# SiLU as one ScalarE function over several strips in the convolutions, the MLP and a gate of a two-layer vision state-space network

## The chip, the cores and the metric

The kernel runs on one core of one Trainium2 chip. The metric is the device time of one execution in microseconds (us), as the median of several executions. Engines are named as in the profile: PE is TensorE's matmul unit and PEld its weight load, DVE is VectorE, ACT is ScalarE, POOL is GpSimd, and SP is the engine that issues the DMAs.

## What is computed

The input is a batch of 8 images of 64x64 positions with 192 channels, all in f32. Two layers follow each other.

- **Layer 0**: a linear projection to 384 + 384 channels; on the first half a 3x3 depthwise convolution and SiLU; a state-space scan in two directions in chunk form, done by matmuls; a gate SiLU(z) of the second half; an output projection with residual; then an MLP 192 -> 768 -> 192 with SiLU between, and a residual.
- **Layer 1**: the first 96 channels go through two 3x3 convolutions and a 1x1 convolution with ReLU. The other 96 are layer-normed and projected to `xi` and `z`, 192 channels each; `xi` has a 3x3 depthwise convolution and SiLU; a selective scan in four directions with 16 states a channel; a layer norm, a gate SiLU(z), and a projection back.

```python
def _silu(v):
    return v * jax.nn.sigmoid(v)
...
xi = jax.nn.silu(_conv(xi, conv2d_w, conv2d_b, groups=D_INNER))
...
def step(h, t):
    u_t, d_t, b_t, c_t = t
    h = jnp.exp(d_t[..., None] * A) * h + (d_t * u_t)[..., None] * b_t[:, :, None, :]
    return (h, jnp.einsum('bkdn,bkn->bkd', h, c_t))
...
yv = _ln(yv, out_norm_g, out_norm_b) * jax.nn.silu(z)
```

SiLU stands in five places: after each of the two depthwise convolutions, in the gate of layer 0, in the MLP and in the gate of layer 1.

## The kernel before

**Rounds.** The work is a pipeline over the 8 images. A round holds up to three parts: `pre` of one image (layer 0 and the preparation of layer 1's scan: stages a to f), `scan` of the image before it (layer 1's selective scan: stage s), and `fin` of the image before that (stages g and h: sum of directions, norm, gate, output projection). There are ten rounds: one with `pre` alone, one with `pre` and `scan`, six in the middle with all three, one with `scan` and `fin`, one with `fin` alone. Between rounds all engines meet at a barrier (`clear`) and semaphores are set to zero.

**The scan** is 384 units of 128x1024 a round. For a unit ACT takes the exponential of the step (`dA<-dA,A`), PE spreads the input over the states into one of two PSUM buffers (`PU<-PT,SELB`), DVE multiplies it by B (`PU<-PU,BR`) and runs the recurrence as a scan instruction (`H<-dA,CR,PU`, line 1738), ACT copies the last state for the chunk that follows (`CR<-H`), POOL multiplies by C (`HC<-H,BR`) and PE sums over the states (`PY<-HC,CB`). The spreading of unit u+1 waits for the scan of unit u-1, since it takes the same half of `PU` (`s_expand`).

**Stages of `pre`.** They work on 8 strips of 512 positions. a: transposes, input projection, and the depthwise convolution, of which PE does six taps (`a.conv`), ACT two (`side_taps`) and DVE one and the merge (`merge_taps`); then SiLU, and from it the tokens (transposes and a projection, `a.tokens`). b: layer 0's chunked scan. c: gate, output projection, and the MLP (`c.mlp`, six blocks of 128 hidden channels a strip, then `c.mlp2`). d: the three convolutions of layer 1. e: norm, `in_proj` (`e.inproj`) and the depthwise convolution (`e.conv`). f: step sizes by softplus and their products.

**The order.** Every engine executes its own fixed list. Generators (`pipeline`, `woven`) write the list of steps of `pre` and `fin`; the table `TAKEN` then says for each kind of round and engine how many of these steps stand behind each third of a scan slot (`merged`). So where a step stands among the scan units is a number in that table, and a late operand holds up all that is behind it on its engine. In a middle round `pre` and `fin` have two PSUM banks for one another's matmuls and evictions at a time (`Round`).

**SiLU before.** v times sigmoid(v) is written as h·(1 + tanh h) with h = v/2. Weights and biases are halved once (`WH`, `DV0`). In the depthwise convolutions ACT computes tanh of `T1` into `T0` (`conv_tanh`), and DVE combines both (`a_silu`, `e_silu`). In the MLP and in layer 1's gate ACT reads the PSUM bank twice, for tanh and for h (`c_mlp`, `e_inproj`), and DVE combines:

```python
act(K.MA[m % 2], pb[:, :], ACT.Tanh, bias=K.DV0[:, 18 + j:19 + j], scale=0.5)
act(K.MB[m % 2], pb[:, :], ACT.Identity, bias=K.DV0[:, 18 + j:19 + j], scale=0.5).then_inc(S["c_hact"], 1)
...
stt(K.HB[i % 2][j], K.MA[m % 2], 1.0, K.MB[m % 2], ADD, MUL).then_inc(S["c_hs"], 1)
```

Layer 0's gate (`c_gate`) has the same form; there DVE multiplies with PSUM directly.

## Time and profile before

| | |
|---|---|
| median of 3 runs | 19261.31 us (19232.4 to 19284.86) |
| profiled execution, its own time | 19287.62 us |
| its span | 19285.8 us |
| PE busy | 14729.8 us, 76% |
| DVE busy | 15816.2 us, 82% |
| ACT busy | 8249.6 us, 43% |
| POOL busy | 10174.2 us, 53% |
| granted TensorE clock, mean | 0.826 of full speed |

Busy times are sums over the whole span, and the rounds have different limits; so a stage is read from its own stretch. A matmul's end is modelled, and a busy PE isn't PE at its peak. The idle time in front of an instruction is put down to what was seen to end it.

### The profile page before, as it was taken

Reading aid. Unit: us, or ns where it says so; the run is one execution under the profiler, and the core shown is the slowest. Engines: PE = TensorE matmul, PEld = TensorE weight load, DVE = VectorE, ACT = ScalarE, POOL = GpSimd, SP = SyncE. Lnnn points to the kernel's source line nnn. Section 1 sums busy time; section 2 is a strip of 40 time slices with the busy share of each in tenths; the row PEclk is TensorE's granted clock in tenths of the full one; section 3 lists DMA queues with packets and bytes.
Section 4 is the critical chain, followed back from the end, with each engine's and each line's share of the span. In section 5 each row is a group of like instructions: output and inputs, shape, how many; then the busy total and the mean of one; then the engine's idle time right before and its main releaser. Section 6 shows DMA issues by size and latency. Waiting matters only on the chain. (4 is left out here: it accounts for less than half of the span.)

```text
span 19285.8 us, 212341 instructions
## 1 busy us (share of the span) xinstructions
PE 14729.8 (76%) x65784; PEld 6341.4 (33%) x65784; DVE 15816.2 (82%) x12143; ACT 8249.6 (43%) x14280; POOL 10174.2 (53%) x5172
## 2 busy tenths in 40 slices
PE   7886789677886788767886878867788678874554
PEld 4433433233332333234332343324333233321102
DVE  3327989689887988979888798988988798898994
ACT  3244334543355334643346433454335533463332
POOL 2115755466455654547455574456645565454662
PEclk9988888788988889888977888878898888975555
DMA  2226666566765667666675666666766566757774
GB/s 80 85 75 174 179 180 168 162 174 186 176 167 166 180 180 187 169 163 182 170 194 163 170 183 177 176 172 174 189 175 167 169 179 180 188 166 175 185 183 113
DMA packets 1556889, 3220.31 MB, mean 167 GB/s; under 512 B 289936, under 2 KB 721872, under 8 KB 1554256
## 3 DMA queue, kind: packets, MB, share of 16 engines
q1 hardware_dynamic: 1555792, 3206.72, 62.4%
q8 instruction: 561, 9.19, 0.2%
q14 instruction: 536, 4.39, 0.1%
HBM read 2474.94 MB, written 731.12 MB: 166 GB/s over the span
## 5 line engine op out<-in xcount | busy, mean ns | idle before, releaser
L1887 POOL TENSOR_TENSOR HC<-H,BR 128x1024 f32<-128x1024 f32 x3072 | 7380.3, 2404 | 5919.5 <-DVE H L1738 3717.3
L1738 DVE TENSOR_TENSOR_SCAN H<-dA,CR,PU 128x1024 f32<-128x1024 f32 x2304 | 5400.1, 2344 | 375.9 <-ACT CR L1119 166.8
L789 PE MATMUL PU<-PT,SELB 96*128 96x512 bf16 x6144 | 2280.3, 460 | 3097.3 <-DVE H L1738 2536.4
L1119 ACT ACTIVATE dA<-dA,A 128x1024 f32<-128x1024 f32 x3072 | 3508.6, 1143 | 2306.2 <-DMA dA<-dld 2280.4
L1482 DVE TENSOR_TENSOR PU<-PU,BR 128x1024 f32<-128x1024 f32 x3072 | 3731.2, 1215 | 411.5 <-PE PU L789 390.3
L789 PE MATMUL PB<-RA,RB 128*128 128x64 f32 (+3 forms) x9120 | 2804.8, 456 | 76.2 <-DVE RA L1485 65.1
L789 PE MATMUL PY<-HC,CB 128*32 128x256 f32 x24576 | 2397.2, 469 | 72.0 <-POOL HC L1887 51.2
L789 PEld LDWEIGHTS PU<-PT,SELB 96*128 96x128 bf16 x6144 | 505.2, 104 | 4675.4 <-issue 4065.7
L1738 DVE TENSOR_TENSOR_SCAN H<-dA,PU 128x1024 f32<-128x1024 f32 x768 | 1755.0, 2285 | 141.1 <-ACT dA L1119 49.3
L789 PEld LDWEIGHTS PB<-RA,RB 128*128 128x128 f32 (+2 forms) x9120 | 1394.6, 188 | 1307.7 <-issue 1173.8
L789 PE MATMUL PB<-RA 128*128 128x384 f32 (+2 forms) x4272 | 1758.1, 551 | 9.0 <-ACT RA L1119 9.0
L1119 ACT ACTIVATE YS<-PY 128x256 f32<-128x256 f32 x768 | 293.2, 382 | 2344.4 <-PE PY L789 2282.7
L789 PEld LDWEIGHTS PB<-RA 128*128 128x128 f32 (+1 forms) x4272 | 870.0, 213 | 944.9 <-issue 762.5
L789 PE MATMUL PB<-RB 96*128 96x128 bf16 (+2 forms) x6624 | 853.3, 260 | 391.5 <-ACT RA L1119 333.2
L789 PE MATMUL PB<-RA,PX 96*128 96x512 f32 x2304 | 1125.3, 629 | 19.4 <-issue 16.0
L1119 ACT ACTIVATE CR<-H 128x1 f32<-128x1 f32 x3072 | 598.0, 195 | 1218.4 <-DVE H L1738 1211.6
L789 PEld LDWEIGHTS PY<-HC,CB 128*32 128x32 f32 x24576 | 530.9, 118 | 1732.5 <-issue 1546.8
L1119 ACT ACTIVATE RA<-PB 128x384 f32<-128x384 f32 (+2 forms) x1736 | 752.9, 457 | 712.9 <-PE PB L789 470.9
L1809 POOL TENSOR_TENSOR T<-T,PX 128x512 f32<-128x512 f32 (+1 forms) x320 | 407.0, 1272 | 929.5 <-ACT PX L1119 929.2
L789 PE MATMUL PB<-XT,RB 96*128 96x512 f32 x1536 | 794.4, 656 | 87.8 <-issue 36.7
L789 PEld LDWEIGHTS PB<-RB 128*128 128x128 f32 (+1 forms) x6624 | 686.2, 153 | 501.4 <-ACT RA L1119 367.9
L1828 POOL TENSOR_TENSOR RA<-RA 128x768 f32<-128x768 f32 x344 | 505.8, 1470 | 594.5 <-PE PB L789 377.4
(174 smaller groups left out, 18145.8 us busy)
## 6 DMA issues: line engine op xcount, KB each, us to landing
dA<-dld SPq DMA_DIRECT2D x3072, 512.0 KB, 6.4
PT<-ptd SPq DMA_DIRECT2D x2304, 64.0 KB, 4.4
BR<-bcd SPq DMA_DIRECT2D x256, 512.0 KB, 7.4
ptd<-RA SPq DMA_DIRECT2D x176, 576.0 KB, 3.9
y0d<-RA SPq DMA_DIRECT2D x512, 192.0 KB, 7.8
RA<-y0d SPq DMA_DIRECT2D x128, 768.0 KB, 6.5
yd<-YS SPq DMA_DIRECT2D x768, 128.0 KB, 4.9
tkd<-RB SPq DMA_DIRECT2D x256, 262.0 KB, 4.8
```

Of the source, the lines that this page charges most:

```text
L789: return nc.tensor.matmul(out, w, x, start=start, stop=stop, skip_group_check=True)
L1119: return ac.activation(out, in_, f, **kw)
L1482: return v.tensor_tensor(out, a, b, op)
L1738: v.tensor_tensor_scan(h, a, x, 0.0 if first else K.CR[:, gi:gi + 1], MUL, ADD).then_inc(S["s_scan"], 1)
L1809: po.tensor_tensor(o, o, K.PX[0:P, strip(m % 3)], ADD).then_inc(S["side"], 1)
L1828: po.tensor_tensor(K.DX[u % 3].rearrange("p (w h q) -> p w h q", w=2, h=6), tk[:, xo:xo + 384].rearrange("p (h q) -> p h q", h=6).unsqueez ...
L1887: po.tensor_tensor(K.HC[:, w % NHC, :], K.H[:, w % NH, :], K.BR[:, (w // 24) % NBR, 1, :], MUL).then_inc(S["s_mulC"], 1)
```

## The change

In the two depthwise convolutions, the MLP and layer 1's gate, the halving is dropped, the pre-activation is written to SBUF whole, and one ACT instruction with the function Silu works in place or into its target over several strips: 1536 columns in stage a (the three channel blocks of a strip), 3072 in the MLP (its six blocks), 1024 in the gate (two blocks), 2048 in stage e (four strips). DVE's combining instructions are gone there. The consumers wait for one such instruction where they waited for three to six. Layer 0's gate stays as it was. Three DMAs of a strip's convolution output go out together behind its one Silu, and the gate's two DMAs become one. The tables of the order are others. The cut diff:

```diff
...
     ("first", "PE"): counts(
-        "0000000000000300300000000600000000600000600000600000600000600000G00900400100100h009006000001001f09005003101009"
...
+        "0000000000000300300000000600000000600000600000600000600000600000G00900400000200h00900600000200000o005003001001"
...
-    "tap": {"a": 24, "e": 16}, "half": {"a": 24, "e": 16}, "tanh": {"a": 24, "e": 16},
-    "silu": {"a": 24, "e": 16},
+    "tap": {"a": 24, "e": 16}, "half": {"a": 24, "e": 16}, "silu": {"a": 8, "e": 4},
...
-        "zo0": {"e": 128}, "zo1": {"e": 128},
+        "zo0": {"e": 64}, "zo1": {"e": 64},
...
-        self.XJ = [rb(512) for _ in range(3)]
+        self.XJS = rb(1536)
+        self.XJ = [self.XJS[:, j * 512:(j + 1) * 512] for j in range(3)]
+        self.TA = [t[:, :, :].rearrange("p j n -> p (j n)") for t in (T0, T1)]
...
-        self.HB = [[ra(512) for _ in range(6)], [PX[:, j * 512:(j + 1) * 512] for j in range(6)]]
+        self.HB = [ra(3072), PX[:, :]]
...
-        self.MA = [XI[:, i, :, :].rearrange("p a c -> p (a c)")[:, 0:512] for i in range(2)]
-        self.MB = [rb(512), ra(512)]
...
-        self.ZT = [ra(512, 96) for _ in range(2)]
-        self.ZO = [XI[0:96, i, :, :].rearrange("p a c -> p (a c)")[:, 0:512] for i in range(2)]
+        self.ZO = [XI[0:96, :, :, :].rearrange("p i a c -> p i (a c)")[:, :, 0:512],
+                   ra(1024, 96).rearrange("p (j n) -> p j n", j=2)]
...
-        pe.wait_ge(*R.at("silu", m + 1, "a"))
+        pe.wait_ge(*R.at("silu", m // 3 + 1, "a"))
...
-            pe.wait_ge(S["c_hs"], 6 * i + 6)
+            pe.wait_ge(S["c_hs"], i + 1)
...
-    def side_taps(ph, m, P, img, w, bias, i):
-        o = K.T1[0:P, m % 3, :]
+    def side_taps(ph, m, P, o, img, w, bias, i):
         o8 = K.PX[0:P, strip(m % 3)]
         if m >= 3:
-            ac.wait_ge(*R.at("silu", m - 2, ph))
-        act(rows8(o), tap_rows(img, i, 7), ACT.Identity, bias=bias, scale=K.WH[0:P, w + 7:w + 8])
-        act(rows8(o8), tap_rows(img, i, 8), ACT.Copy, scale=K.WH[0:P, w + 8:w + 9]).then_inc(S["taps"], 1)
-
-    def conv_tanh(ph, m, P):
-        ac.wait_ge(*R.at("half", m + 1, ph))
-        if m >= 3:
-            ac.wait_ge(*R.at("silu", m - 2, ph))
-        act(K.T0[0:P, m % 3, :], K.T1[0:P, m % 3, :], ACT.Tanh).then_inc(S["tanh"], 1)
+            ac.wait_ge(*R.at("side", m - 2, ph))
+        act(rows8(o), tap_rows(img, i, 7), ACT.Identity, bias=bias, scale=K.V[0:P, w + 7:w + 8])
+        act(rows8(o8), tap_rows(img, i, 8), ACT.Copy, scale=K.V[0:P, w + 8:w + 9]).then_inc(S["taps"], 1)
 
     def a_side(m, p):
         i, j = divmod(m, 3)
         if m == 0:
             ac.wait_ge(*R.at("rim", 1, "a"))
         ac.wait_ge(S["a_rows"], 3 * min(i + 1, 7) + 3)
-        side_taps("a", m, 128, K.XP[:, j], 9 * j, K.DV0[:, 15 + j:16 + j], i)
-
-    def a_conv(m, tap):
-        if tap == NTAP:
-            conv_tanh("a", m, 128)
+        if i >= 2:
+            ac.wait_ge(*R.at("silu", i - 1, "a"))
+        side_taps("a", m, 128, K.TA[i % 2][:, strip(j)], K.XP[:, j], W0 + 9 * j, K.vec("cb", j, P=128), i)
+
+    def a_silu(m, p):
+        i, j = divmod(m, 3)
+        if p or j < 2:
+            return
+        ac.wait_ge(*R.at("half", m + 1, "a"))
+        if i:
+            ac.wait_ge(S["a_tproj"], 4 * i)
+            for j in range(3):
+                ac.wait_ge(S[f"xj{j}"], 16 * i)
+        act(K.XJS, K.TA[i % 2], ACT.Silu).then_inc(S["silu"], 1)
...
     def c_mlp(i, j):
         m = 6 * i + j
-        pb = R.bank(("c.mlp", i, j))
+        if i >= 2:
+            ac.wait_ge(S["c_mlp"], 2 * (i - 2) + 2)
         ac.wait_ge(S["c_h"], m + 1)
-        if m >= 2:
-            ac.wait_ge(S["c_hs"], m - 1)
-        act(K.MA[m % 2], pb[:, :], ACT.Tanh, bias=K.DV0[:, 18 + j:19 + j], scale=0.5)
-        act(K.MB[m % 2], pb[:, :], ACT.Identity, bias=K.DV0[:, 18 + j:19 + j], scale=0.5).then_inc(S["c_hact"], 1)
+        act(K.HB[i % 2][:, strip(j)], R.bank(("c.mlp", i, j))[:, :], ACT.Identity,
+            bias=K.vec("b1", j, P=128)).then_inc(S["c_hact"], 1)
+        if j == 5:
+            ac.wait_ge(S["c_hact"], m + 1)
+            act(K.HB[i % 2], K.HB[i % 2], ACT.Silu).then_inc(S["c_hs"], 1)
...
-            m = 2 * i + e - 2
-            if m >= 2:
-                ac.wait_ge(S["e_z"], m - 1)
-                ac.wait_ge(S[f"zo{m % 2}"], 16 * (m // 2))
-            act(K.ZT[m % 2], pb[0:96, :], ACT.Tanh, bias=K.IPW[:, 4 + e:5 + e], scale=0.5)
-            act(K.ZO[m % 2], pb[0:96, :], ACT.Identity, bias=K.IPW[:, 4 + e:5 + e], scale=0.5).then_inc(S["e_zact"], 1)
+            zo = K.ZO[i % 2]
+            if i >= 2:
+                ac.wait_ge(S[f"zo{i % 2}"], 16 * (i // 2))
+            act(zo[:, e - 2, :], pb[0:96, :], ACT.Identity, bias=K.IPW[:, e:e + 1]).then_inc(S["e_zact"], 1)
+            if e == 3:
+                ac.wait_ge(S["e_zact"], 2 * i + 2)
+                act(zo, zo, ACT.Silu).then_inc(S["e_z"], 1)
 
     def e_side(m, p):
         j, i = divmod(m, 8)
         ac.wait_ge(S["e_rows"], 2 * min(i + 1, 7) + 2)
-        side_taps("e", m, 96, K.YP[:, j], 27 + 9 * j, K.DV0[0:96, 24 + j:25 + j], i)
-
-    def e_conv(m, tap):
-        if tap == NTAP:
-            if m == 0:
-                ac.wait_ge(S["e_p"], 32)
-            conv_tanh("e", m, 96)
+        if m == 0:
+            ac.wait_ge(S["e_xn"], 8)
+        side_taps("e", m, 96, K.C1[:, j, strip(i)], K.YP[:, j], W1 + 9 * j, K.vec("cdb", j), i)
+
+    def e_silu(m, p):
+        j, i = divmod(m, 8)
+        if i % 4 == 3:
+            x = K.C1[:, j, (i - 3) * 512:(i + 1) * 512]
+            ac.wait_ge(*R.at("half", m + 1, "e"))
+            act(x, x, ACT.Silu).then_inc(S["silu"], 1)
...
-    def merge_taps(ph, m, P, pb, img, w, i):
-        x = K.T1[0:P, m % 3, :]
+    def merge_taps(ph, m, P, x, pb, img, w, i):
         v.wait_ge(*R.at("conv", m + 1, ph))
         v.wait_ge(*R.at("side", m + 1, ph))
-        stt(rows8(x), tap_rows(img, i, 6), K.WH[0:P, w + 6:w + 7], rows8(x), MUL, ADD).then_inc(S["tap"], 1)
+        stt(rows8(x), tap_rows(img, i, 6), K.V[0:P, w + 6:w + 7], rows8(x), MUL, ADD).then_inc(S["tap"], 1)
         v.wait_ge(*R.at("tap", m + 1, ph))
         tt(x, x, pb[0:P, :], ADD).then_inc(S["half"], 1)
 
...
-    def a_silu(m, p):
-        if p:
-            return
-        i, j = divmod(m, 3)
-        v.wait_ge(*R.at("tanh", m + 1, "a"))
-        if i:
-            v.wait_ge(S["a_tproj"], 4 * i)
-            v.wait_ge(S[f"xj{j}"], 16 * i)
-        stt(K.XJ[j], K.T0[:, m % 3, :], 1.0, K.T1[:, m % 3, :], ADD, MUL).then_inc(S["silu"], 1)
+            merge_taps("a", m, 128, K.TA[i % 2][:, strip(j)], R.bank(("a.conv", m, 0)), K.XP[:, j], W0 + 9 * j, i)
...
-    def c_mlp(i, j):
-        m = 6 * i + j
-        v.wait_ge(S["c_hact"], m + 1)
-        if i >= 2:
-            v.wait_ge(S["c_mlp"], 2 * (i - 2) + 2)
-        stt(K.HB[i % 2][j], K.MA[m % 2], 1.0, K.MB[m % 2], ADD, MUL).then_inc(S["c_hs"], 1)
-
...
-    def e_inproj(i, e):
-        if e >= 2:
-            m = 2 * i + e - 2
-            v.wait_ge(S["e_zact"], m + 1)
-            stt(K.ZO[m % 2], K.ZT[m % 2], 1.0, K.ZO[m % 2], ADD, MUL).then_inc(S["e_z"], 1)
-
...
-            merge_taps("e", m, 96, R.bank(("e.conv", m, 0)), K.YP[:, j], 27 + 9 * j, i)
-
-    def e_silu(m, p):
-        j, i = divmod(m, 8)
-        v.wait_ge(*R.at("tanh", m + 1, "e"))
-        if m == 0:
-            v.wait_ge(S["e_xn"], 8)
-        stt(K.C1[:, j, strip(i)], K.T0[0:96, m % 3, :], 1.0, K.T1[0:96, m % 3, :], ADD, MUL).then_inc(S["silu"], 1)
+            merge_taps("e", m, 96, K.C1[:, j, strip(i)], R.bank(("e.conv", m, 0)), K.YP[:, j], W1 + 9 * j, i)
...
-        if p == 1:
-            sp.wait_ge(*R.at("silu", m + 1, "a"))
-            dma(K.xc0[j, :, strip(i)], K.XJ[j], f"xj{j}")
+        if p == 1 and j == 2:
+            sp.wait_ge(*R.at("silu", i + 1, "a"))
+            for j in range(3):
+                dma(K.xc0[j, :, strip(i)], K.XJ[j], f"xj{j}")
...
-        if e >= 2:
-            m = 2 * i + e - 2
-            sp.wait_ge(S["e_z"], m + 1)
-            dma(K.zd[par, e - 2, :, strip(i)], K.ZO[m % 2], f"zo{m % 2}")
+        if e == 3:
+            sp.wait_ge(S["e_z"], i + 1)
+            dma(K.zd[par, :, :, strip(i)].rearrange("j p n -> p j n"), K.ZO[i % 2], f"zo{i % 2}")
...
```

**The order on two engines.** In the rows below `T<-PB` is the tanh of layer 0's gate, `dA<-dA,A` and `CR<-H` belong to scan units, and `YS<-PY` is a result of the scan. First ACT in stage c of a middle round, at the MLP of one strip; before:

```order
L1119 ACTIVATE T<-PB 128x512
L1119 ACTIVATE XI<-PB,DV 128x512
L1119 ACTIVATE RA<-PB,DV 128x512
L1119 ACTIVATE XI<-PB,DV 128x512
L1119 ACTIVATE RB<-PB,DV 128x512
L1119 ACTIVATE YS<-PY 128x256
L1119 ACTIVATE dA<-dA,A 128x1024
L1119 ACTIVATE CR<-H 128x1
```

and of the changed kernel:

```order
L1118 ACTIVATE T<-PB 128x512
L1118 ACTIVATE RA<-PB,V 128x512
L1118 ACT_TABLE_LOAD
L1118 ACTIVATE RA<-RA 128x3072
L1118 ACTIVATE PX<-PB,V 128x512
L1118 ACTIVATE YS<-PY 128x256
L1118 ACT_TABLE_LOAD
L1118 ACTIVATE dA<-dA,A 128x1024
L1118 ACTIVATE CR<-H 128x1
```

Each block's pair of PSUM reads (`XI`, `RA` or `RB`) became one read into the strip's buffer; behind the sixth stand a table load, the Silu of 3072 columns, and a table load ahead of the next exponential.

DVE in the same stage, before (`RA<-XI,RB` and its like combine tanh and h in the MLP; `T` rows are the gate; the row named L1738 is the scan instruction):

```order
L1485 SCALAR_TENSOR_TENSOR RA<-T 128x512
L1485 SCALAR_TENSOR_TENSOR RA<-XI,RB 128x512
L1485 SCALAR_TENSOR_TENSOR T<-T,PB 128x512
L1482 TENSOR_TENSOR PU<-PU,BR 128x1024
L1738 SCALAR_TENSOR_TENSOR H<-dA,PU 128x1024
L1485 SCALAR_TENSOR_TENSOR RA<-XI,RA 128x512
L1485 SCALAR_TENSOR_TENSOR T<-RB,DV,PB 128x512
L1485 SCALAR_TENSOR_TENSOR RA<-T 128x512
L1485 SCALAR_TENSOR_TENSOR PX<-XI,RB 128x512
```

and of the changed kernel, where the scan is L1704:

```order
L1482 SCALAR_TENSOR_TENSOR RA<-T 128x512
L1482 SCALAR_TENSOR_TENSOR T<-T,PB 128x512
L1482 SCALAR_TENSOR_TENSOR T<-RB,DV,PB 128x512
L1482 SCALAR_TENSOR_TENSOR RA<-T 128x512
L1479 TENSOR_TENSOR RA<-PB,XT 96x512
L1479 TENSOR_TENSOR PU<-PU,BR 128x1024
L1704 SCALAR_TENSOR_TENSOR H<-dA,PU 128x1024
L1479 TENSOR_TENSOR PU<-PU,BR 128x1024
L1704 SCALAR_TENSOR_TENSOR H<-dA,PU 128x1024
```

The combining rows are gone from DVE, and more scan units stand between a strip's other work: in a middle round DVE has 51, 135, 62, 66, 42 and 28 units in the stages a to f before, and 49, 136, 70, 65, 40 and 24 in the changed kernel.

ACT in stage e, `in_proj` (`RA<-PB,IPW 96x512` was tanh and is now the plain read of a block; `XI<-PB,IPW` was h), before:

```order
L1119 ACTIVATE RA<-PB,IPW 96x8x64 x2
L1119 ACTIVATE YS<-PY 128x256
L1119 ACTIVATE dA<-dA,A 128x1024
L1119 ACTIVATE CR<-H 128x1
L1119 ACTIVATE RA<-PB,IPW 96x512
L1119 ACTIVATE XI<-PB,IPW 96x512
```

and of the changed kernel:

```order
L1118 ACTIVATE RA<-PB,IPW 96x512
L1118 ACT_TABLE_LOAD
L1118 ACTIVATE RA<-RA 96x1024
L1118 ACTIVATE RA<-PB,IPW 96x8x64 x2
L1118 ACT_TABLE_LOAD
L1118 ACTIVATE dA<-dA,A 128x1024
```

Here too a Silu stands between two table loads. Over the whole program ACT has 133 table loads before and 479 in the changed kernel.

## Rows read from the trace of the kernel before

**Rows 1.** The page, part 1: busy us, share of the span, instructions.
```profile
PE 14729.8 (76%) x65784; PEld 6341.4 (33%) x65784; DVE 15816.2 (82%) x12143; ACT 8249.6 (43%) x14280; POOL 10174.2 (53%) x5172
```
**Rows 2.** Windows, one a round: stretch, its length, busy us of each engine, clock.
```profile
0.00:1536.00 1536.00, 1170.80 (x4003) 593.55 (x4003) 514.68 (x695) 509.01 (x861) 333.05 (x285) 0.90 0.28 84
1536.00:3704.00 2168.00, 1733.59 (x7839) 733.97 (x7839) 1883.01 (x1427) 978.12 (x1720) 1241.65 (x638) 0.86 0.65 173
...
8298.00:10593.00 2295.00, 1810.98 (x8223) 790.05 (x8223) 1986.16 (x1515) 1028.99 (x1788) 1277.39 (x646) 0.85 0.66 175
...
17467.00:18971.00 1504.00, 871.77 (x4212) 209.51 (x4212) 1433.95 (x855) 544.15 (x919) 922.26 (x391) 0.52 0.72 182
```
**Rows 3.** Windows, the six stages a to f of one middle round.
```profile
8298.00:8619.00 321.00, 280.59 (x1229) 133.36 (x1230) 229.38 (x175) 156.05 (x325) 149.88 (x75) 0.94 0.62 170
8619.00:9286.00 667.00, 493.08 (x3157) 271.06 (x3149) 627.88 (x548) 249.40 (x501) 460.73 (x264) 0.85 0.67 179
9286.00:9682.00 396.00, 349.84 (x1292) 131.29 (x1292) 336.62 (x279) 153.60 (x262) 177.43 (x70) 0.93 0.63 170
9682.00:10051.00 369.00, 318.15 (x1352) 139.93 (x1347) 319.80 (x222) 144.78 (x235) 178.09 (x75) 0.81 0.80 198
10051.00:10284.00 233.00, 206.42 (x725) 63.93 (x724) 215.45 (x170) 133.48 (x216) 127.86 (x78) 0.83 0.55 144
10284.00:10593.00 309.00, 162.90 (x488) 50.48 (x488) 257.02 (x125) 191.67 (x251) 183.39 (x87) 0.72 0.61 177
```
**Rows 4.** Page, part 5: the scan unit's instructions on DVE and PE.
```profile
L1738 DVE TENSOR_TENSOR_SCAN H<-dA,CR,PU 128x1024 f32<-128x1024 f32 x2304 | 5400.1, 2344 | 375.9 <-ACT CR L1119 166.8
L789 PE MATMUL PU<-PT,SELB 96*128 96x512 bf16 x6144 | 2280.3, 460 | 3097.3 <-DVE H L1738 2536.4
L1482 DVE TENSOR_TENSOR PU<-PU,BR 128x1024 f32<-128x1024 f32 x3072 | 3731.2, 1215 | 411.5 <-PE PU L789 390.3
L789 PE MATMUL PY<-HC,CB 128*32 128x256 f32 x24576 | 2397.2, 469 | 72.0 <-POOL HC L1887 51.2
L1738 DVE TENSOR_TENSOR_SCAN H<-dA,PU 128x1024 f32<-128x1024 f32 x768 | 1755.0, 2285 | 141.1 <-ACT dA L1119 49.3
```
**Rows 5.** Waits of PE in one round: stage a, then c, then e.
```profile
PE PU L789 <- DVE H L1738: 34.1, 19, 9.2
...
PE PU L789 <- DVE H L1738: 33.3, 19, 6.3
...
PE PU L789 <- DVE H L1738: 20.1, 13, 2.9
```
**Rows 6.** Groups by shape, DVE: the instructions that combine tanh and h.
```profile
L1485 DVE SCALAR_TENSOR_TENSOR RB<-T 128x512 f32<-128x512 f32 x192 | 166.0, 868 | 55.6 <-PE PB L789 55.4
L1485 DVE SCALAR_TENSOR_TENSOR XI<-RA,XI 96x512 f32<-96x512 f32 x128 | 148.0, 1189 | 25.7 <-ACT XI L1119 25.6
L1485 DVE SCALAR_TENSOR_TENSOR RA<-XI,RA 128x512 f32<-128x512 f32 x96 | 111.1, 1158 | 91.7 <-ACT RA L1119 91.2
L1485 DVE SCALAR_TENSOR_TENSOR PX<-XI,RA 128x512 f32<-128x512 f32 x96 | 108.2, 1127 | 66.2 <-ACT RA L1119 65.9
L1485 DVE SCALAR_TENSOR_TENSOR RA<-XI,RB 128x512 f32<-128x512 f32 x96 | 99.4, 1035 | 26.2 <-ACT RB L1119 25.6
L1485 DVE SCALAR_TENSOR_TENSOR RB<-T 96x512 f32<-96x512 f32 x128 | 98.5, 773 | 0.1
L1485 DVE SCALAR_TENSOR_TENSOR PX<-XI,RB 128x512 f32<-128x512 f32 x96 | 84.1, 876 | 32.8 <-ACT RB L1119 32.4
```
**Rows 7.** Groups by shape, ACT: tanh in a and MLP, table loads, widths of 1024 and 4096.
```profile
L1119 ACT ACTIVATE XI<-PB,DV 128x512 f32<-128x512 f32 x384 | 263.9, 687 | 784.3 <-PE PB L789 783.8 <-DVE RA L1485 0.5
L1119 ACT ACT_TABLE_LOAD x115 | 147.5, 1283 | 181.7 <-PEq L2219 162.9 <-DMA tkd<-RB 17.1
L1119 ACT ACTIVATE T<-T 128x512 f32<-128x512 f32 x192 | 120.9, 630 | 618.2 <-DVE T L1482 618.2
L1119 ACT ACTIVATE RA<-RA 96x1024 f32<-96x1024 f32 x96 | 94.9, 1045 | 0.1
L1119 ACT ACTIVATE RB<-RB 96x4096 f32<-96x4096 f32 x8 | 28.8, 3603 | 0.0
```
**Rows 8.** Timeline of ACT in stage f, around one softplus stretch: start us, us.
```profile
10373.66 1.06 ACT L1119 ACTIVATE RA<-RA 96x1024 bf16<-96x1024 f32 x1 [1.44 <-DVE RA L1482]
10374.74 1.28 ACT L1119 ACT_TABLE_LOAD   x1
10376.03 2.00 ACT L1119 ACTIVATE RA<-RA 96x1024 f32<-96x1024 f32 x2
...
10382.72 1.28 ACT L1119 ACT_TABLE_LOAD   x1
10384.01 1.15 ACT L1119 ACTIVATE dA<-dA,A 128x1024 f32<-128x1024 f32 x1
```
**Rows 9.** Waits of DVE in stage f, until 10520 us.
```profile
DVE PU L1482 <- PE PU L789: 9.9, 2, 7.0
DVE H L1738 <- ACT CR L1119: 3.2, 1, 3.2
```

More of the change, by code:

```diff
@@ L39 @@
 NTAP = 6
+W0, W1 = VCOL["w0"][0], VCOL["w1"][0]
 UNITS = [(k, c, d, g) for k in range(4) for c in (range(4) if k < 2 else range(3, -1, -1))
@@ L472 @@
            "g_y13 g_all h_n h_g h_gate h_mm h_copy "
-           "rim diag taps side conv tap half tanh silu mean xm sq var vr rstd").split()
+           "rim diag taps side conv tap half silu mean xm sq var vr rstd").split()
 DMAS = {"weights": None, "xt0": None, "xt1": None,
@@ L743 @@
 ENDS = {
-    "a": [("a_tk", 64), ("a_tproj", 32), ("b_dve", 1), ("silu", 24), ("side", 24), ("xT", 0), ("a_turn", 16),
-          ("a_proj", 24), ("tanh", 24)],
+    "a": [("a_tk", 64), ("a_tproj", 32), ("b_dve", 1), ("silu", 8), ("side", 24), ("a_turn", 16),
+          ("a_proj", 24)],
     "b": [("b_ysum", 64), ("b_y", 64), ("b_state", 64), ("b_dx", 64), ("b_cb", 64), ("b_exp", 128)],
-    "c": [("c_x1", 16), ("c_mlp", 16), ("c_hs", 48), ("c_yg", 0), ("c_ysum", 8)],
+    "c": [("c_x1", 16), ("c_mlp", 16), ("c_hs", 8), ("c_ysum", 8)],
     "d": [("d_xl", 8), ("d_c3", 8)],
-    "e": [("silu", 16), ("conv", 16), ("side", 16), ("e_z", 16), ("e_p", 32)],
+    "e": [("silu", 4), ("conv", 16), ("side", 16), ("e_z", 8), ("e_p", 32)],
     "h": [("h_copy", 16), ("h_mm", 16), ("h_gate", 16)],
@@ L1255, in e_begin @@
             ac.wait_ge(S["e_b"], 1)
-            act(K.IPW[:, 0:4], pb[0:96, 0:4], ACT.Copy)
-            act(K.IPW[:, 4:8], pb[0:96, 0:4], ACT.Copy, scale=0.5).then_inc(S["e_ipb"], 1)
+            act(K.IPW[:, :], pb[0:96, 0:4], ACT.Copy).then_inc(S["e_ipb"], 1)
     def e_mean(i, p):
@@ L1785, in h_gates @@
             tt(o, o, K.ZB[:, strip(j)], MUL).then_inc(S["h_gate"], 1)
-    do = {"a.begin": a_begin, "a.conv": a_conv, "a.silu": a_silu, "b.setup": b_setup, "b.mix": b_mix, "b.out": b_out,
-          "c.begin": c_begin, "c.gate": c_gate, "c.outp": c_outp, "c.mlp": c_mlp, "c.mlp2": c_mlp2,
-          "d.begin": d_begin, "e.begin": e_begin, "e.mean": e_mean, "e.norm": e_norm, "e.inproj": e_inproj,
-          "e.conv": e_conv, "e.silu": e_silu, "f.begin": f_begin, "f.split": f_split, "s": s_slot,
+    do = {"a.begin": a_begin, "a.conv": a_conv, "b.setup": b_setup, "b.mix": b_mix, "b.out": b_out,
+          "c.begin": c_begin, "c.gate": c_gate, "c.outp": c_outp, "c.mlp2": c_mlp2,
+          "d.begin": d_begin, "e.begin": e_begin, "e.mean": e_mean, "e.norm": e_norm,
+          "e.conv": e_conv, "f.begin": f_begin, "f.split": f_split, "s": s_slot,
           "g.total": g_total, "g.mean": g_mean, "h.gates": h_gates}
@@ L1811, in a_side @@
     def a_side(m, p):
-        side("a", m, 128)
+        i, j = divmod(m, 3)
+        side("a", m, 128, K.TA[i % 2][:, strip(j)])
     def b_setup(_, p):
@@ L1863, in e_begin @@
             for i in range(18):
-                po.tensor_scalar(K.DG1[:, i, :], K.IDENT[0:96, 0:96], K.WH[0:96, 27 + i:28 + i], 1.0,
+                po.tensor_scalar(K.DG1[:, i, :], K.IDENT[0:96, 0:96], K.V[0:96, W1 + i:W1 + i + 1], 1.0,
                                  MUL, MUL).then_inc(S["diag"], 1)
     def e_side(m, p):
-        side("e", m, 96)
+        j, i = divmod(m, 8)
+        side("e", m, 96, K.C1[:, j, strip(i)])
     def f_begin(_, p):
```

256 lines of the change are left out of this document (122 added, 134 removed).

## The prediction

> **What bounds the kernel now.** I read the page's busy shares first: DVE 82%, PE 76%, ACT 43% [rows 1]. No engine is full, so the next view is the stretches. By round [rows 2] the eight rounds with a scan hold nearly all the time: one of 2168 us, six of about 2295 us (one stands for all) and one of 1504 us. The round with `pre` alone takes 1536 us at a DVE share of a third, and PE's 1171 us leads there. The 1504 us round holds none of the changed code. So the change is decided in seven rounds.
>
> Within one middle round [rows 3] the stages differ. In b DVE is busy 628 of 667 us. In a, c and e PE leads or is level: 281 of 321, 350 of 396, 206 of 233 us, with DVE at 229, 337 and 215. These three are the stages that the change touches. A scan unit costs DVE (5400 + 1755 + 3731)/3072 = 3.54 us and PE (2280 + 2397)/3072 = 1.52 us [rows 4]. What does PE wait for in a, c and e? Nearly all is one thing, the spreading of a unit behind the scan two units before: 34.1, 33.3 and 20.1 us [rows 5], of 40, 46 and 27 us idle. So PE's own work sets the length there, and DVE adds through that wait: 87.5 us a round. The reader should see that DVE's 82% doesn't make a microsecond off DVE a microsecond off the end.
>
> **What is removed.** DVE loses 832 combining instructions: 166.0 + 148.0 + 111.1 + 108.2 + 99.4 + 98.5 + 84.1 = 815.3 us [rows 6], or 102 us in each of eight rounds: 21 in a, 50 in c, 31 in e. ACT loses 832 tanh instructions: 192 of 630 ns, 384 of 687 ns [rows 7], and 128 + 128 in layer 1 that I take at the same two values, 554 us together.
>
> **What is added.** 28 Silus a round. From widths 1024 and 4096 [rows 7] a column costs (3603 - 1045)/3072 = 0.833 ns on a base of 192 ns. So 1536, 3072, 1024 and 2048 columns take 1.47, 2.75, 1.05 and 1.90 us, and 64 + 64 + 64 + 32 of them 398 us. Table loads go from 133 to 479 in the order of ACT's instructions: 346 x 1.283 us [rows 7] = 444 us. ACT ends at 8250 - 554 + 398 + 444 = 8540 us, 44% to 45%: not the bound by its sum.
>
> Is a switch of tables 1.283 us, or more? Around a softplus stretch the load starts 0.02 us after the instruction before it ended, and the next one starts as it ends [rows 8]. So I take 1.283. The Trainium skill (ScalarE: Activation LUTs, "What ACT_TABLE_LOAD costs") adds about 1380 ns of drain for 2.66 us a switch; by that ACT would gain 920 us, and end at 47%; this trace doesn't show the drain.
>
> **What of it lies on the path.** Per middle round, stage by stage; the table of the order also moves scan units between stages.
> - a, 51 to 49 units: PE's work 281 - 2 x 1.52 = 278. PE's wait for scans is 34 now. DVE is 21 us lighter; I let half of that come off the wait. Why half: between nothing and all 21 the rows give no measure. Against all of it speaks that DVE in stage a is busy only 71% and PE waits there anyway; for some of it, that the combining rows stand between scans. 278 + 24 + 6 other = 308, 13 less.
> - c, 62 to 70 units: PE 350 + 8 x 1.52 = 362, wait 33 - 25 = 8, other 13: 383, 13 less, with eight more units done.
> - e, 42 to 40 units: PE 203, wait 20 - 15 = 5, other 7: 215, 18 less.
> - b one unit more, d one less: 0 together. f has four units less, and DVE leads there [rows 3]: 4 x 3.54 = 14 less.
>
> That is 58 us a round. On the other side stand the ACT stretches: a Silu with its two loads holds ACT for 3.6 to 5.3 us, in which no exponential and no eviction runs, and PE has two banks for `pre`. Nearest rows: the softplus stretches of stage f, where 9.3 us pass from the first load to the next exponential [rows 8], while DVE's waits on ACT in that stage are 3.2 us in all [rows 9]. So exponentials run ahead far enough. Evictions are less covered, since PE is full in c and e. Bounds: nothing, and both loads, 2.57 us a Silu. I take 0.5 us, nearer the low end as rows 9 are: 28 x 0.5 = 14 us a round. Work moved to other semaphores, the one DMA for the gate and the three in one go for the convolution cost nothing: their targets are read in later stages. If that cover went, the next strip's Silu would wait for the landing, as its code says. The halving that goes from setup is a few small instructions, nothing.
>
> 58 - 14 = 44 us. The 2168 us round loses the same 102 us of DVE work and has the same stages; I take the same. 7 x 44 = 308 us. The round with `pre` alone gets 0: PE leads and its consumers of Silu are a stage later. 19,287.6 - 308 = 18,980 us against the profiled execution; that one stands 26 us above the median shown, so 18,954, rounded to 18,950, 1.6% faster. A measurement of this kernel tells about 0.3% (58 us) from no change.
>
> **The rivals.**
> - **PE's waits stay.** The wait comes from the alternation of spreading and scan over two buffers and from long runs of matmuls, not from DVE's load. For it: stage a, with the least loaded DVE, has as long a wait as c [rows 3, 5]. Then the 50 us that I took off the waits stay; 58 - 50 - 14 = -6 us a round, and the time is 19,261 + 42 = 19,300, no change to be told. DVE's idle time grows by what it lost. Chance 0.13.
> - **ACT's stretches land on the path (slower).** Place: stages c and e, where one Silu, its loads and the evictions of its strip stand between two groups of exponentials; PE stands for a bank, then DVE for PE. Price: 2.57 us a Silu where I took 0.5, so 72 us a round, 19,387 - 26 = 19,360, 0.5% slower. It decides from 2.1 us a Silu on ((44 + 14)/28). Against it: [rows 8, 9]. Chance 0.11. The skill's rule in the same page ("Table sets: the hidden batching unit") is to batch activations by set, and the change does the opposite by switching 346 times more; at its 2.66 us a switch this rival would cost 149 us a round and end near 19,900, which is part of that chance.
> - **DVE's work comes off whole.** If DVE were the bound through the coupling, 102 us a round: 7 x 102 = 714, 18,574 - 26 = 18,550. For it: DVE at 0.87 of a middle round, more than PE's 0.79 [rows 2]. Against it: PE's own 350 of 396 us in c. Chance 0.10.
> - That the change doesn't do what it says is small: combining rows are gone and the loads are there in the order. A chance of its own isn't needed.
>
> **How the numbers follow.** Forecast 0.66, waits stay 0.13, slower 0.11, whole 0.10. The forecast's own range: recovered share between a quarter and three quarters of 102 us (25 more or less a round) and a price of 0 to 1.2 us a Silu: about 18,700 to 19,200. The range reaches to 19,240, to take in part of the second case, and leaves out the whole recovery and the slower case, 2 in 10. Faster 0.66 + 0.10 = 0.76, same 0.13, slower 0.11.
>
> **What the profile after should show.** DVE busy near 15,000 us; ACT near 8540 with 479 loads of 1283 ns and Silus of 1.05 to 2.75 us. The six middle rounds near 2250 us; stage c near 383 us with 70 units, PE's wait for scans in it under 15 us. If that wait is still 30 us, the first rival holds. If PE or DVE waits for ACT by over 40 us a round, the second does. If middle rounds are near 2190 us, the last. A TensorE clock in c and e far from 0.93 and 0.83 [rows 3] would make PE's terms wrong.

## The result, and the profile after

The changed kernel takes 19122.59 us (median of 4 runs, 19115.85 to 19140.05) against 19265.76 us of the kernel before (19232.4 to 19284.86). The ratio is 0.9929, with a 95% interval of 0.9912 to 0.9946: 0.7% faster. The forecast was 18,950 us, 1.6% faster. The sign is right and the time lies in the range, but only about half of the expected gain came: 143 us of 311 by the medians, 165 us of 308 by the profiled executions (19,287.6 and 19,122.3 us).

The page of the changed kernel, part 1 (busy us, share of the span, instructions), as [rows 1]:

```profile
PE 14690.5 (77%) x65784; PEld 6360.6 (33%) x65784; DVE 15166.5 (79%) x11306; ACT 8601.2 (45%) x14010; POOL 10124.7 (53%) x5172
```

DVE is 650 us less busy, not 815. ACT is at 8601 us where 8540 were worked out. Windows of the changed kernel, one a round for the first, the second and one middle round, as [rows 2] (stretch, length, busy us of PE, PEld, DVE, ACT, POOL, granted clock, DMA share, GB/s):

```profile
0.00:1517.00 1517.00, 1161.52 (x4003) 585.85 (x4003) 447.75 (x585) 498.33 (x785) 336.93 (x285) 0.90 0.28 85
1517.00:3628.00 2111.00, 1692.73 (x7839) 722.48 (x7839) 1816.48 (x1322) 1031.90 (x1695) 1244.18 (x638) 0.88 0.66 178
...
8202.00:10479.00 2277.00, 1789.90 (x8223) 788.24 (x8223) 1901.75 (x1410) 1080.49 (x1759) 1267.93 (x646) 0.86 0.66 177
```

Over the six middle rounds the mean goes from 2293.9 to 2279.6 us. So the 165 us are 6 x 14.3 = 86 from the middle rounds, 57 from the first round with a scan, 19 from the round with `pre` alone (forecast 0) and the few left from the last two rounds. The forecast had 44 us from each middle round. That is where the gain is missing. The stages a to f of that middle round, as [rows 3]:

```profile
8202.00:8507.00 305.00, 277.75 (x1206) 133.56 (x1210) 209.64 (x147) 172.51 (x319) 144.98 (x73) 0.93 0.62 173
8507.00:9192.00 685.00, 493.37 (x3167) 272.11 (x3167) 633.85 (x550) 252.49 (x504) 463.53 (x265) 0.85 0.66 176
9192.00:9603.00 411.00, 370.16 (x1372) 138.77 (x1372) 318.59 (x249) 175.86 (x255) 191.58 (x78) 0.91 0.66 177
9603.00:9977.00 374.00, 308.30 (x1334) 137.11 (x1338) 309.55 (x219) 145.63 (x236) 176.11 (x82) 0.84 0.82 197
9977.00:10190.00 213.00, 185.79 (x704) 59.57 (x696) 194.31 (x133) 149.08 (x205) 121.40 (x67) 0.92 0.53 141
10190.00:10479.00 289.00, 154.53 (x448) 47.13 (x448) 235.80 (x116) 184.93 (x243) 170.32 (x85) 0.74 0.63 184
```

As means over the six middle rounds, with the scan units done in each stage:

| stage | units | us before | us after | moved | forecast |
|---|---|---|---|---|---|
| a | 51, 49 | 317.5 | 304.7 | -13 | -13 |
| b | 135, 136 | 665.2 | 683.3 | +18 | 0 |
| c | 62, 70 | 398.8 | 411.7 | +13 | -13 |
| d | 66, 65 | 372.7 | 373.8 | +1 | 0 |
| e | 42, 40 | 231.1 | 217.1 | -14 | -18 |
| f | 28, 24 | 308.6 | 289.1 | -20 | -14 |

The forecast also set 14 us a round aside for ACT's stretches. Two stages fail, b and c, by 18 and 26 us a round. What PE waits for in them, as [rows 5] (waits of PE in this round, stage a, then c, then e; us, times, longest):

```profile
PE PU L788 <- DVE H L1704: 27.5, 11, 9.1
...
PE PU L788 <- DVE H L1704: 38.8, 17, 4.8
...
PE PU L788 <- DVE H L1704: 21.0, 15, 3.1
```

In c the wait should have fallen from 33 to 8 us. It is 38.8 here and 40 over the middle rounds. DVE is busy 319 of 411 us there, 18 us less than before with eight scan units more, and the stage is 13 us longer over the middle rounds.

### The profile page after: what moved, and what is told of

Read it like the earlier page. It is cut to its first block and busy times, and to the rows that moved or that the text cites. A ratio compares the mean times of both kernels' runs of the same rounds, so it can differ in the third digit from the quotient of the medians.

```text
span 19120.1 us, 210423 instructions
## 1 busy us (share of the span) xinstructions
PE 14690.5 (77%) x65784; PEld 6360.6 (33%) x65784; DVE 15166.5 (79%) x11306; ACT 8601.2 (45%) x14010; POOL 10124.7 (53%) x5172
## 5 line engine op out<-in xcount | busy, mean ns | idle before, releaser
L1854 POOL TENSOR_TENSOR HC<-H,BR 128x1024 f32<-128x1024 f32 x3072 | 7305.8, 2380 | 5971.9 <-DVE H L1704 3556.5
L1704 DVE TENSOR_TENSOR_SCAN H<-dA,CR,PU 128x1024 f32<-128x1024 f32 x2304 | 5402.5, 2345 | 285.7 <-ACT CR L1118 71.3
L788 PE MATMUL PB<-RA,RB 128*128 128x64 f32 (+3 forms) x9120 | 2808.6, 457 | 28.0 <-DVE RA L1482 15.7
L1704 DVE TENSOR_TENSOR_SCAN H<-dA,PU 128x1024 f32<-128x1024 f32 x768 | 1755.4, 2286 | 144.6 <-ACT dA L1118 51.3
L788 PE MATMUL PB<-XT,RB 96*128 96x512 f32 x1536 | 833.4, 683 | 71.1 <-DMA XT<-xTd 29.9
L788 PE MATMUL PB<-T,RA 128*128 128x512 f32 (+1 forms) x1024 | 594.0, 705 | 191.2 <-ACT RA L1118 76.4
```

Source lines behind the costliest of these rows:

```text
L788: return nc.tensor.matmul(out, w, x, start=start, stop=stop, skip_group_check=True)
L1704: v.tensor_tensor_scan(h, a, x, 0.0 if first else K.CR[:, gi:gi + 1], MUL, ADD).then_inc(S["s_scan"], 1)
L1854: po.tensor_tensor(K.HC[:, w % NHC, :], K.H[:, w % NH, :], K.BR[:, (w // 24) % NBR, 1, :], MUL).then_inc(S["s_mulC"], 1)
```

## Why DVE's saving is not PE's saving: reading the slots

A slot is one place in the table of the order, with one scan unit or part of one and the steps beside it. Two stretches of stage c of the kernel before, as windows: three units with nothing beside them, and a run of MLP and gate steps.

```profile
9289.00:9300.00 11.00, 6.39 (x35) 1.10 (x38) 10.68 (x7) 0.63 (x2) 7.56 (x4) 0.50 1.02 297
...
9400.00:9432.00 32.00, 30.78 (x103) 12.51 (x102) 17.57 (x21) 10.79 (x18) 6.75 (x3) 1.00 0.43 124
```

And like stretches of the changed kernel; the first row is a run of stage a, the other two are the same two kinds in stage c:

```profile
8295.00:8330.00 35.00, 35.00 (x100) 15.98 (x99) 11.48 (x13) 14.28 (x22) 9.79 (x8) 1.00 0.22 64
...
9195.00:9206.00 11.00, 6.39 (x35) 1.10 (x38) 10.68 (x7) 2.64 (x5) 7.55 (x4) 0.50 1.01 299
...
9299.00:9332.00 33.00, 32.94 (x107) 13.34 (x106) 12.74 (x17) 10.25 (x12) 3.26 (x2) 1.00 0.37 104
```

Where units stand alone, DVE is busy 10.68 of 11 us, PE 6.39, and PE waits; no combining row stood there, and the two kernels agree to the last digit on PE and DVE. The run of MLP and gate steps had six combining rows on DVE before and has none after: there PE is busy for nearly the whole stretch (30.78 of 32 us, 32.94 of 33), and DVE went from 17.57 to 12.74 us at nearly the same length. Much of DVE's relief fell where it had slack.

How far that goes can be counted over the six middle rounds, by what DVE did in the 7.5 us before each of PE's waits for a scan in c. Of 32.6 us a round before the change, 15.7 stood behind scan units alone, 8.1 behind combining rows and 8.8 behind other steps. Of 39.7 us after it, 15.5 stand behind units alone and 24.2 behind other steps. So the part behind lone units is untouched, and what went behind combining rows came back, and more, behind the other steps.

## The experiments

All ratios are against the kernel before, measured beside each run. Three theories for the missing gain were tried against one another, and the expectations call them A, B and C. A: the Silu stretches with their table loads land on the path. B: PE's waits don't follow DVE's load. C: the new order costs time in stages whose code did not change.

### x1: Tanh in the place of Silu

```diff
-        act(K.XJS, K.TA[i % 2], ACT.Silu).then_inc(S["silu"], 1)
+        act(K.XJS, K.TA[i % 2], ACT.Tanh).then_inc(S["silu"], 1)
```

The same in the MLP, the gate and the second convolution. It computes tanh instead of SiLU, in the same places and shapes, without the 346 further loads.

> The changed kernel with the function Tanh where it has Silu, at the same widths and places: the output isn't SiLU, but Tanh stands in the same table set as Exp, so the added table loads are gone and nothing else moves. Changed kernel: 19,123 us. Theory A (ACT's stretches with their loads are where the expected gain went, mostly in the middle rounds, which gained 14 us each and not 44): 18,900 us or less, with stage c back from 412 to under 395 us. Theory B (PE's wait for scans doesn't shrink when DVE gets lighter, loads are covered): 19,080 to 19,130 us. Theory C (the moved scan units and the other order cost it): 19,080 to 19,130 us.

Measured: 19088.99 us, ratio 0.9902 [0.9888, 0.9917]. Stage c of one middle round, as a window:

```profile
9146.00:9556.00 410.00, 368.31 (x1372) 138.34 (x1372) 319.03 (x249) 155.74 (x239) 191.59 (x78) 0.91 0.68 177
```

ACT's busy time falls to 8143.3 us, 458 less, and the end moves by 34 us by the medians (52 by the ratios). Stage c keeps its 410 us. That comes to 0.10 to 0.15 us at the end for each load of 1.283 us, and even this is near the noise: the interval meets that of the changed kernel. The loads are not where the gain went.

### x5: no activation to speak of

```diff
-        act(K.XJS, K.TA[i % 2], ACT.Silu).then_inc(S["silu"], 1)
+        act(K.XJS[:, 0:8], K.TA[i % 2][:, 0:8], ACT.Tanh).then_inc(S["silu"], 1)
```

The same at the other three places. Everything past the first 8 columns is left without an activation; a memset at the start fills one of the targets.

> The changed kernel with Tanh on 8 columns in the place of every Silu (the activation of the other columns is left out): the 346 loads and nearly all of the Silus' 398 us are gone from ACT, the order stays. It prices all that the change adds to ACT. The same with full width was 19,089 us (34 us under the changed kernel). Theory A (ACT's stretches hold the end): 19,000 us or less. Theories B and C (they are covered): 19,060 to 19,095 us.

Measured: 19068.67 us, 0.9891 [0.9876, 0.9905]; ACT 7810.6 us. Stage c of one middle round:

```profile
9146.00:9553.00 407.00, 366.54 (x1368) 137.21 (x1372) 318.13 (x248) 135.89 (x238) 190.64 (x78) 0.92 0.67 178
```

All that the change adds on ACT costs 54 us of the end by the medians, 73 by the ratios. The forecast had 7 x 14 = 98. Stage c goes from 411 to 407 us in this round and from 411.7 to 409.2 over the six, though next to nothing of a Silu is left in it. Theory A falls.

### x2: the kernel before, without the combining

```diff
-        stt(K.XJ[j], K.T0[:, m % 3, :], 1.0, K.T1[:, m % 3, :], ADD, MUL).then_inc(S["silu"], 1)
+        stt(K.XJ[j][:, 0:8], K.T0[:, m % 3, 0:8], 1.0, K.T1[:, m % 3, 0:8], ADD, MUL).then_inc(S["silu"], 1)
```

The same at the other three places, 832 instructions in the old order; two memsets at the start set what is then never written. The product past column 8 is left out. This is the forecast's step "half of DVE's saving comes off PE's waits" by itself.

> The kernel before, its own order, with each of the 832 combining instructions of DVE cut to 8 columns (the products are left out but for these; two small memsets in setup, some 4 us): DVE loses about 650 us, ACT and the order stay. Kernel before: 19,266 us. It prices the DVE work alone. Theory B (PE's wait stays, DVE isn't what holds the end in stages a, c and e): 19,200 to 19,260 us. Forecast's step (half of DVE's saving comes off): 18,940 to 19,000 us. DVE is the bound: 18,650 us.

Measured: 19191.23 us, 0.9958 [0.9942, 0.9975], with DVE's busy time 469 us lower (15346.9). Stage c of one middle round, as a window, and then PE's wait in it:

```profile
9237.00:9635.00 398.00, 355.67 (x1292) 134.18 (x1292) 308.69 (x281) 154.40 (x263) 172.53 (x70) 0.92 0.63 170
```
```profile
PE PU L789 <- DVE H L1740: 30.2, 16, 5.4
```

DVE loses 28 us in this stage and the wait falls by 3; the mean of c over the middle rounds goes from 398.8 to 394.7. Over the kernel 0.42% comes off, some 81 to 88 us: a sixth of the saving, not half. The time lies 9 us under the range of theory B and 190 above that of the forecast's step. The test is smaller than meant: with 8 columns the 832 instructions still hold DVE for part of their time, so 469 us went and not 650. What came, came mainly in e (231.1 to 222.3 us), and there it is two things: the wait for scans falls by 5.5 us, and PE's busy time for the same matmuls by 4.8 (203.2 to 198.4), at a granted clock of 0.87 where it was 0.85.

### x3: the MLP by tanh in the new order

```diff
-        act(K.HB[i % 2][:, strip(j)], R.bank(("c.mlp", i, j))[:, :], ACT.Identity,
-            bias=K.vec("b1", j, P=128)).then_inc(S["c_hact"], 1)
-        if j == 5:
-            ac.wait_ge(S["c_hact"], m + 1)
-            act(K.HB[i % 2], K.HB[i % 2], ACT.Silu).then_inc(S["c_hs"], 1)
+        act(K.MA[m % 2], pb[:, :], ACT.Tanh, bias=K.DV0[:, 18 + j:19 + j], scale=0.5)
+        act(K.MB[m % 2], pb[:, :], ACT.Identity, bias=K.DV0[:, 18 + j:19 + j], scale=0.5).then_inc(S["c_hact"], 1)
...
+        stt(K.HB[i % 2][:, strip(j)], K.MA[m % 2], 1.0, K.MB[m % 2], ADD, MUL).then_inc(S["c_hs"], 1)
```

The bias halved at the start and the counts of `c_hs` come back with it; the order stays the new one.

> The changed kernel in its own order, with the MLP alone back in the old form (two reads of each block on ACT, 384 combining instructions on DVE, no Silu of 3072 columns and none of its loads). Changed kernel: 19,123 us. Theory A (the loads and the Silu of the MLP cost stage c its gain): 19,030 to 19,090 us, stage c under 400 us in middle rounds. Theory B (DVE and ACT both have room in stage c): within 30 us of 19,123. Forecast's step (25 us of DVE work a round comes off in c): 19,200 to 19,300 us.

Measured: 19403.38 us, 1.0069 [1.0054, 1.0084], 280 us above the changed kernel, slower than the kernel before, and 103 us above the highest range expected. The mean of c is 445.2 us. Stage c of one middle round, and PE's waits in it:

```profile
9306.00:9750.00 444.00, 377.51 (x1368) 140.39 (x1372) 359.70 (x296) 160.62 (x278) 195.20 (x78) 0.89 0.61 163
```
```profile
PE PU L790 <- DVE H L1713: 45.1, 21, 5.1
PE PB L790 <- DVE RA L1484: 14.8, 8, 7.0
PE PB L790 <- DVE PX L1484: 7.7, 1, 7.7
```

DVE is 41 us busier and the stage 33 us longer. In the old order, with 62 units, 28 us off DVE gave 4 (x2); in the new one, with 70, 41 us on DVE cost 33. So the new order of c cannot carry the old form of the MLP. But this is not a price of DVE's load alone. PE waits 22.5 us for `RA` and `PX`, the products that DVE combines, where its two waits of this kind in c of the changed kernel were 1.7 and 1.6 us: the combining stands between ACT's reads and the MLP's second product again, and in places of DVE's list that hold no work in the changed kernel. How much of the 33 us is load and how much is this chain the run does not separate.

### x4: the old order for stage b

```diff
+RULES = {'middle': {'b': 0}}
...
+        if step[0][0] in rules:
+            at = min(max(other[step] + 3 * rules[step[0][0]], 0), len(slots))
```

In the middle rounds the steps of b stand in the slots of the table before; all else is the changed kernel.

> The changed kernel with stage b's steps in the six middle rounds at the slots that the kernel before has for them; a and c to f stay. Stage b does the same work in both kernels but takes 683 us on average in the middle rounds of the changed one and 665 before, with one unit more. Theory C (the other order costs it, also where no code changed): b back to 665 to 670 us, 19,030 to 19,060 us. Theories A and B: b's length comes from what precedes it; within 30 us of 19,123.

Measured: 19024.55 us, 0.9872 [0.9858, 0.9887]. Stages b and c of one middle round:

```profile
8450.00:9115.00 665.00, 493.84 (x3159) 271.64 (x3159) 632.84 (x549) 252.22 (x504) 462.90 (x265) 0.85 0.69 180
9115.00:9528.00 413.00, 365.42 (x1372) 137.24 (x1372) 318.56 (x249) 176.30 (x254) 190.90 (x78) 0.91 0.67 177
```

The mean of b goes from 683.3 back to 667.7 us with c at 413.0. The time is 98 us less than that of the changed kernel by the medians, 69 by the profiled executions, of which x4's is the slowest of its four and has d 3 us a round longer; it is 1.3% under the kernel before. Theory C holds for b. Busy times of b are those of the changed kernel (DVE 632.84 against 633.85), so what the other order costs there is waiting, not work. This version beats both kernels.

Which waiting, the traces tell. Waits in stage b of one middle round in the changed kernel, of PE and then of DVE:

```profile
PE PB L788 <- ACT RA L1118: 73.5, 43, 5.6
PE PU L788 <- DMA PT<-ptd: 10.3, 2, 9.0
...
DVE RA L1479 <- PE PB L788: 27.2, 22, 4.2
DVE PU L1479 <- PE PU L788: 6.2, 1, 6.2
```

And in x4:

```profile
PE PB L1011 <- ACT RA L1341: 49.6, 32, 3.6
...
DVE RA L1702 <- PE PB L1011: 17.3, 20, 3.3
```

DVE is the fuller engine in b, and it stands idle for 51 of 685 us in the changed kernel and for 32 of 665 in x4. Of these 19 us, 10 are waits for b's own matmuls, whose banks wait longer for ACT's reads (`RA`), and 6 are a wait for the spreading of one unit, which itself waits for a load (`PT<-ptd`). In each of the six middle rounds of the changed kernel PE waits 4 to 9 us for that load, 64 us into b; in b of the kernel before and of x4 it never waits for one.

### x6: the old order for b and c

```diff
+RULES = {'middle': {'b': 0, 'c': 0}}
```

> As x4_old_order_b (19,025 us), with stage c's steps in the middle rounds also at the old slots: 62 units in it, and the seven slots up to stage d then hold scan units alone. Theory B (in c the length is PE's, and Silu instead of the DVE work buys next to nothing at an unchanged order): the old slots of c take 393 to 399 us (399 before, 395 with the combining gone), the seven after it 25 us, so 418 to 424 us against 413, and 19,055 to 19,100 us. Forecast's step (25 us of waits come off in c): the old slots under 380 us, below 19,000 us.

Measured: 19145.85 us, 0.9935 [0.9921, 0.995], 46 us above the range expected. The old slots of c, and then the units behind them that the old order does not use for c, in one middle round:

```profile
9163.00:9560.00 397.00, 353.41 (x1292) 133.73 (x1292) 291.47 (x229) 168.60 (x239) 172.64 (x70) 0.92 0.64 170
9560.00:9585.00 25.00, 14.20 (x74) 2.37 (x70) 24.20 (x19) 9.23 (x17) 16.38 (x8) 0.50 0.73 180
```

In its old slots c takes 394 to 399 us, 396 on average against 398.8 before the change, with DVE at 291 instead of 337: 45 us off DVE, and 2 off the stage. (The Silus and their loads are in it too; x5 prices them at 2.5 us in c of the new order.) The units left over then run alone, with DVE busy 24.20 of 25 us. From the same slot to the same slot that is 429.4 us against 413 in x4, so 16 us a round is what it earns to stand eight more units in c. That accounts for 98 of the 121 us between x6 and x4 by the medians (of 101 by the profiled executions). The expectation missed because one slot at the start of c was left out of it, worth 6 to 7 us a round; the rest is open.

### x7: x4 with the steps of c spread evenly

```diff
+EVEN = {'middle': {'c': (193, 216)}}
...
+        for step, cost in zip(steps, costs):
+            at[step] = 3 * int(lo + (hi - lo) * done / total) + 2
+            done += cost
```

The steps of c that PE has in the slots 193 to 215 are spread over these slots, each in one slot on every engine, by its share of PE's work, to take away the stretches where units stand alone and the runs without them.

> x4_old_order_b with the steps of stage c that PE has in slots 193 to 215 of the middle rounds spread evenly over these slots, by their cost, on all engines; the new order has them in runs of up to 33 us with three scan units between. Theory B (PE's waits stand in slots that hold scan units alone, where DVE has nothing but 3.54 us a unit; grouping makes such slots): PE's wait for scans in c falls from 43 to under 30 us, c from 413 to 400 us, 18,930 to 18,990 us. If the waits have another cause: 19,010 to 19,040 us.

Measured: 19627.07 us, 1.0187 [1.017, 1.0204]. Stage c of one middle round as a window, and the waits of PE and DVE in it:

```profile
9337.00:9844.00 507.00, 398.66 (x1372) 150.44 (x1372) 317.52 (x249) 176.70 (x255) 191.87 (x78) 0.85 0.54 144
```
```profile
PE PU L1027 <- DVE H L1943: 82.8, 33, 6.1
...
DVE T L1721 <- ACT T L1357: 80.4, 21, 15.3
```

A clear miss: c grows by 97 us at unchanged work. The edit also put each step on all engines into the same slot, where the table has the consumers stand later, so DVE now waits 80.4 us for ACT and PE 82.8 for the scans. What this kernel shows is the worth of the lead that the engines have over one another; of the grouping by itself it shows nothing.

### x8 and x9: lighter work on one engine in c

```diff
-            t = mm(pb[:, :], K.w1[:, k, j * 128:(j + 1) * 128], xo[:, k * 512:(k + 1) * 512], k == 0, k == 1)
+            t = mm(pb[:, 0:256], K.w1[:, k, j * 128:(j + 1) * 128], xo[:, k * 512:k * 512 + 256], k == 0, k == 1)
```

x8 leaves out half the columns of the MLP's first product.

> The changed kernel with the MLP's first matmuls on 256 of 512 columns (half of that product is left out; the reads stay as wide): 96 matmuls a round at half length, some 0.33 us each, 31 us of PE's time a round in stage c, order unchanged. Changed kernel 19,123 us. Theory B (PE holds stage c): c falls by 20 to 31 us in each round, 18,870 to 18,970 us. If DVE or ACT holds c: above 19,060 us.

```diff
-            stt(K.YG[j], t0, 0.5, t1, MUL, MUL).then_inc(S["c_yr"], 1)
+            stt(K.YG[j][:, 0:8], t0[:, 0:8], 0.5, t1[:, 0:8], MUL, MUL).then_inc(S["c_yr"], 1)
```

x9 leaves out all but 8 columns of the gate's last product.

> The changed kernel with the last product of layer 0's gate on 8 of 512 columns (24 instructions of 0.86 us a round, 19 us of DVE's time a round in stage c are left out), order unchanged. The mirror of x8. Theory B: c falls by 0 to 5 us a round, 19,080 to 19,125 us. If DVE held c: c falls by 15 us or more, below 19,010 us.

Measured: x8 18982.6 us, 0.985 [0.9833, 0.9866]; x9 19103.84 us, 0.9913 [0.9898, 0.9928]. Stage c of a middle round in x8, and PE's wait in it:

```profile
9093.00:9490.00 397.00, 342.46 (x1372) 141.21 (x1372) 318.21 (x248) 175.70 (x255) 191.44 (x78) 0.87 0.69 182
```
```profile
PE PU L788 <- DVE H L1704: 51.0, 27, 5.8
```

And in x9:

```profile
9167.00:9572.00 405.00, 365.70 (x1372) 137.82 (x1372) 306.19 (x249) 176.12 (x254) 191.48 (x78) 0.92 0.67 179
```

27 us off PE give 15 (20 to 31 were expected, and the time is 13 us above its range) and turn 12 into waits for the scans. 12 us off DVE give 6, at the edge of what was expected (0 to 5). Over the six rounds c goes from 411.7 to 397.0 and 405.8 us. So about half of what either engine loses comes off c, and neither holds the stage alone. Two things weaken this. The granted clock in c was 0.91 in the changed kernel, 0.87 in x8 and 0.92 in x9. And in x9 PE's wait for the scans did not fall (39.7 to 39.1 us a round) while its busy time did, by 4.2 us; at the end x9's interval meets that of the changed kernel. x8's whole gain also takes in the other rounds, the one with `pre` alone among them (1482 us).

## Why the prediction was partly right

- **DVE loses 815 us.** The rows went, yet DVE fell by 650. The groups that join two products cost 141 us more, as the last section shows, and part of the 815 was waiting for POOL. The step counted only what left.
- **ACT's sum and its path price.** 479 loads of 1283 ns and Silus of 1.48, 2.76 and 1.91 us stand in the groups of the changed kernel, against 1.47, 2.75 and 1.90 worked out. The price on the path, 98 us, measured 54 to 73 (x5): near enough, and on the careful side. The slower rival fell by x5, not by the sign set for it: PE waits for ACT 118 us a round in the changed kernel, over the 40 named, but it waited 80 before the change and still waits 113 in x5. The reading of [rows 9] was too narrow as well: they end at 10520 us, and over all of stage f DVE waits 10.5 us for ACT, not 3.2.
- **a, e and f.** 308, 215 us and 14 less were forecast for one round; 305, 213 and about 20 less came. The lengths are right, the terms behind two of them are not, and that is luck. Over the six rounds e was to lose 3 us of PE's work and 15 of its wait for scans; it lost 9.9 (203.2 to 193.3) and 5.4 (21.4 to 16.0). Two units are worth 3 of the 9.9; the granted clock, which the forecast held, was 0.89 where it had been 0.85, and 0.92 against 0.83 in the round shown. a was to lose 3 and 10 us; it lost 0.7 and 5.9, and the rest came off small waits that the forecast had left as they were.
- **c: "wait 33 - 25 = 8".** This is the step that failed. The wait is 40 us, and c is 412 us, not 383. "Half of DVE's saving comes off PE's waits" was chosen between bounds from averages of a stage; x2 and x6 give 4 and 2 us for 28 and 45 us off DVE in the old order. The slots give a reason that fits, though no run tests it by itself: much of DVE's relief fell where PE was full, and the waits behind lone units stayed. PE's added work was mis-sized a little too (370 us against 362 in the round shown).
- **b: "one unit more, d one less: 0 together".** The second failure, a stage whose code did not change but whose order did: it was put at nothing with no reason beyond the count of units. It grew 18 us a round; x4 gets 16 back, 98 us by the medians, of the 168 by which the medians miss the forecast.
- **The first round with a scan and the one with `pre` alone** were better than said, by 13 and 19 us; no run looks into why.
- **The rival "PE's waits stay"** was right about the mechanism in c and wrong in its sum, because it kept the waits of a and e as well. Its sign, a wait of still 30 us in c, came true.
- **Where the gain comes from.** DVE's freed time lets eight more units stand under c's matmuls in place of slots in a, e and f (16 us a round, x6 against x4), and with the MLP in its old form the same order is 280 us worse (x3). In the old order the lighter DVE was worth 81 to 88 us (x2), and the work added on ACT cost 54 to 73 in the new one (x5). So more of the gain seems to come through the order than from DVE's load; but that is an estimate across runs. No run has the new code with every stage in its old slots; with b to f there, the engines wait for one another without end.
- **The range.** By its own terms (25 us a round either way, and 0 to 1.2 us a Silu) it would run from about 18,670 to 19,270 us, not 18,700 to 19,200. The measured time lies in both.

Left open: why the load in b lands late, how x3's 33 us divide between DVE's load and the chain, and the part of x6 that the moved slots do not explain.

## What to carry to other kernels

Time taken off an engine counts in the stretches where that engine is the one waited for, so look where the removed instructions stand before giving a share of them to a wait: a stage's mean of 85% hides stretches at 97% and at 55%. Freed time can still be earned by filling it, and then the gain has to be priced as the work that moves in, not as the work that left. Where a table of the order is made anew, every stage in it may change, and each is to be priced or timed by itself, also where its code is the same.
